# Attention unrolled over all sixteen slots, with the causal mask and the maxima's split on VectorE and the weighing one key step at a time

## The reference

```python
B, T, C = x.shape            # 4, 2048, 256
H, hd, L = 16, 16, 32        # heads, head width, latent width
q, k, v = split(x @ c_attn_w.T + c_attn_b)            # 16 heads of 16
q_lat, k_lat, v_lat = q @ q2l_w.T + b, k @ kv2l_w.T + b, v @ kv2l_w.T + b
q_lat, k_lat = rotary(q_lat), rotary(k_lat)
att = einsum('bhql,bhkl->bhqk', q_lat @ wqk_w.T + wqk_b, k_lat) * L ** -0.5
att = where(causal, att, -inf)
att = softmax(att, axis=-1)  # over the keys
y_lat = einsum('bhqk,bhkl->bhql', att, v_lat)
```

## Time and profile before

| what | value |
|---|---|
| median of three runs | 3400.84 us |
| profiled execution: its time / its span | 3398.39 / 3396.8 us |
| mean granted TensorE clock | 0.946 of full speed |
| `project_heads` | 0 to about 445 us |
| `attend`, first max unit to last turned sums | 466 to 2450 us |
| busy: PE, DVE, ACT, POOL | 90%, 69%, 56%, 23% |
| busy in attention (420 to 2340 us): PE, DVE, ACT, POOL | 96%, 77%, 61%, 9% |

### The profile page before, as it was taken

The page is one execution under the profiler, slowest core; times in us unless marked ns, Lnnn a source line. Parts: engine busy times, 40 slices in busy tenths (PEclk is TensorE's granted clock), DMA queues, the critical chain, the costliest instruction groups (busy, mean ns, idle before and its releaser), DMA issues. The chain is left out here.

```text
span 3396.8 us, 62788 instructions
## 1 busy us (share of the span) xinstructions
PE 3042.3 (90%) x17753; PEld 1998.0 (59%) x17753; DVE 2329.9 (69%) x4664; ACT 1909.4 (56%) x3720; POOL 772.3 (23%) x700
## 2 busy tenths in 40 slices
PE   7888869999999999999999999999889996788780
PEld 6677735555555555555555555555467775677670
DVE  7999977777877877877777777777634443343433
ACT  4566616656666656666656656666545453444434
POOL 6777820000000100000000010000025542222120
PEclk9999959999999999999999999999989998899895
DMA  6666662323322332432333233233283212322215
GB/s 221 219 223 225 216 175 69 72 50 72 71 68 53 73 70 48 95 70 49 72 72 72 48 72 71 54 88 72 51 290 119 92 57 71 90 61 71 43 19 204
DMA packets 254481, 333.42 MB, mean 98 GB/s; under 512 B 57074, under 2 KB 146523, under 8 KB 252896
## 3 DMA queue, kind: packets, MB, share of 16 engines
q1 hardware_dynamic: 236512, 306.49, 31.6%
q0 software_dynamic: 17664, 23.19, 3.6%
HBM read 189.90 MB, written 149.19 MB: 100 GB/s over the span
## 5 line engine op out<-in xcount | busy, mean ns | idle before, releaser
L765 DVE TENSOR_REDUCE att_partial_max<-att_max_bank 128x1 f32<-128x512 f32 (+2 forms) x2640 | 1449.3, 603 | 405.2 <-PE att_max_bank L613 313.3
L728 ACT ACTIVATE att_probs<-att_score_bank 128x512 f32<-128x512 f32 (+3 forms) x2560 | 1203.9, 536 | 745.1 <-PE att_score_bank L653 711.6
L653 PE MATMUL att_score_bank<-att_q_st,att_k_st 98*128 98x512 f32 (+3 forms) x2563 | 1030.4, 407 | 29.7 <-issue 29.7
L613 PE MATMUL att_max_bank<-att_k_st,att_q_st 96*128 96x512 f32 (+2 forms) x2640 | 989.8, 384 | 30.1 <-DVE att_ident_b L757 24.6
L653 PEld LDWEIGHTS att_score_bank<-att_q_st,att_k_st 98*128 98x128 f32 x2563 | 496.3, 194 | 498.1 <-ACT att_probs L728 353.2
L669 PE MATMUL att_acc_bank<-att_probs,att_v_st 128*32 128x512 f32 (+3 forms) x5120 | 605.7, 545 | 0.0
L613 PEld LDWEIGHTS att_max_bank<-att_k_st,att_q_st 96*128 96x128 f32 x2640 | 514.2, 195 | 140.9 <-DVE att_partial_max L765 49.8
L749 POOL TENSOR_SCALAR_AFFINE_SELECT att_probs<-att_probs 128x512 f32<-128x512 f32 x256 | 162.4, 634 | 1818.1 <-ACT att_probs L728 1818.1
L211 POOL TENSOR_TENSOR proj_op_low<-proj_turned,proj_op_high 128x512 fp32r<-128x512 f32 x192 | 274.8, 1461 | 59.0 <-ACT proj_op_high L340 58.6
L616 PE MATMUL att_max_bank<-att_mask,att_ident_b 128*128 128x128 bf16 x1066 | 252.5, 237 | 0.0
L616 PEld LDWEIGHTS att_max_bank<-att_mask,att_ident_b 128*128 128x128 bf16 x1066 | 106.6, 100 | 157.2 <-issue 112.5
(11 more groups left out here) (225 smaller groups left out, 3934.0 us busy)
## 6 DMA issues: line engine op xcount, KB each, us to landing
qk_parts<-proj_parts SPq DMA_DIRECT2D x64, 1024.0 KB, 4.6
att_q_st<-qk_parts SPq DMA_DIRECT2D x204, 256.0 KB, 3.9
att_k_st<-qk_parts SPq DMA_DIRECT2D x204, 256.0 KB, 5.9
att_v_st<-v_tokens SPq DMA_DIRECT2D x68, 256.0 KB, 6.7
v_tokens<-proj_v_tok SPq DMA_DIRECT2D x64, 256.0 KB, 4.5
exp_w<-in_ew SPq DMA_DIRECT2D x16, 1024.0 KB, 9.1
dispatched<-mix_empty_rows SPq DMA_DIRECT2D x8, 1036.0 KB, 15.0
exp_rows<-dispatched SPq DMA_DIRECT2D x16, 518.0 KB, 3.7
```

The costliest lines, as they stand in the source:

```text
L613: last = nc.tensor.matmul(out[:, 0:width], q_st[0:3 * L, c, j, t * P:(t + 1) * P], k_st[0:3 * L, par, kb, j, 0:width], start=True, stop=(k ...
L653: nc.tensor.matmul(score_ps[h % (HG * NK) % 3][:, q0:CH], k_st[:, p, kt // TT, j, (kt % TT) * P:(kt % TT + 1) * P], q_st[:, c, j, q0:CH], ...
L728: nc.scalar.activation(probs[:, k % 4, j, q0:CH], score_ps[(HG * k + j) % 3][:, q0:CH], ACT.Exp).then_inc(exped, 1)
L765: nc.vector.tensor_reduce(partial_max[:, m % 2, j * TT + t, kb:kb + 1], max_ps[max_bank(u)][:, 0:width], AX.X, ALU.max).then_inc(unit_redu ...
```

## The change

In `project_heads` the zeros are no longer written. `attend` is written anew:

- no loop: all 640 key steps of the 16 slots stand in the program one after another, and every wait compares with a constant;
- the mask matmul is gone. A diagonal unit's maximum is taken on VectorE by `tensor_tensor_reduce`, which adds a row of 0 and -1e30 (`edge`) and takes the maximum in one pass. In the program this is two instructions: the pass, and one that writes out the accumulator (128x1);
- the transposition of the maxima by TensorE is gone. VectorE splits (`high_max`, `low_max`) and transposes 32x32 blocks (`turn_max`), one small instruction after each of the next three units, and SP writes the shift by eight DMAs in place of two;
- the max units are dealt by columns: `pace_maxima` lists for each score how many units are issued before it, so that columns of units and columns of scores keep step. 48 units stand before the first score, the lead grows to about 90, and nothing is computed beyond slot 16;
- `weigh(k)` now stands after the third score of step k+1 (`AHEAD = 3`), not after the fourth; `probs` has two buffers, not four; `q_st` is a ring of six chunks; the sums alternate between two banks `acc`, are turned in place and divided from there, and `misc` is gone.

```diff
-KS = [(p, c, kt) for p in range(2) for c in range(NC) for kt in range(TT * (c + 1))]
...
-PER_STEP = MUG // KSG
-LEAD = 5 * HG * TT
...
+KS = [(s, c, kt) for s in range(SLOTS) for c in range(NC) for kt in range(TT * (c + 1))]
+MU = [(s, c, j, t, kb) for s in range(SLOTS) for c in range(NC) for j in range(HG) for t in range(TT) for kb in range(c + 1)]
...
+ACCS = 2
+MAXB = 3
+SCOREB = 3
+PROBS = 2
+QBUF = 6
+AHEAD = 3
+TURN_AFTER = 3
+MARGIN = 20
+FIRST_UNITS = 24
+DIVIDE_BACK = 2
...
+    step = [weight_score(*KS[h // HG]) for h in range(NS)]
+    unit = [weight_unit(*m) for m in MU]
+    rate = sum(unit) / sum(step)
...
+    for h in range(NS):
+        while u < NU and unit_sum[u] < start + rate * step_sum[h]:
+            u += 1
+        due[h] = max(needed[h], min(u, FIRST_UNITS + 2 * h))
...
         @block.tensor
...
-                if kb == c:
-                    last = nc.tensor.matmul(out[:, width - P:width], ident_b[:], mask[:], start=False, stop=True)
...
+            def weigh(k):
...
+                pe.wait_ge(exped, HG * (k + 1))
+                if kt >= TT * c:
+                    pe.wait_ge(masked, n * TT + (kt - TT * c) + 1)
+                if kt == 0 and n >= ACCS:
+                    pe.wait_ge(y_done, n - ACCS + 1)
...
+            pe.wait_ge(consts_in, 32)
             pe.wait_ge(ones_set, 1)
-            with pe.Fori(0, ITS) as it:
...
+            for h in range(NS):
+                while u < MAXIMA_BEFORE[h]:
+                    max_unit(u)
+                    u += 1
+                score(h)
+                while weighed < NK and h == min(HG * PAIR * (weighed // PAIR + 1) + AHEAD, NS) - 1:
+                    weigh(weighed)
+                    weighed += 1
...
         @block.vector
...
+                if kb < c:
+                    nc.vector.tensor_reduce(best, bank[:], AX.X, ALU.max).then_inc(unit_reduced, 1)
+                else:
+                    width = (t + 1) * P
+                    dve.sem_inc(masked_max_due, 1)
+                    nc.vector.tensor_tensor_reduce(
+                        out=edge_sum[:, u % MAXB, 0:width], in0=bank[:, 0:width], in1=edge[:, CH - width:CH], scale=1.0, scalar=LEAST,
+                        op0=ALU.add, op1=ALU.max, accum_out=best).then_inc(unit_reduced, 1)
```

More of the change, by code:

```diff
@@ new lines, in pace_maxima, with weight_unit, weight_score @@
+def pace_maxima():
+    def weight_unit(s, c, j, t, kb):
+        return CH if kb < c else (t + 1) * P
+    def weight_score(s, c, kt):
+        return CH - max(kt - TT * c, 0) * P
+    step = [weight_score(*KS[h // HG]) for h in range(NS)]
+    unit = [weight_unit(*m) for m in MU]
+    rate = sum(unit) / sum(step)
+    needed = [0] * NS
+    for n in range(CHUNKS):
+        for h in range(max(HG * FIRST_STEP[n] - MARGIN, 0), NS):
+            needed[h] = UNITS_THROUGH[n]
+    done, due, ahead = 0, [0] * NS, 0
+    unit_sum = [0]
+    for w in unit:
+        unit_sum.append(unit_sum[-1] + w)
+    step_sum = [0]
+    for w in step:
+        step_sum.append(step_sum[-1] + w)
+    slot = len(KS) // SLOTS * HG
+    start = max(unit_sum[needed[h]] - rate * step_sum[h] for h in range(2 * slot, (SLOTS - 2) * slot))
+    u = 0
+    for h in range(NS):
+        while u < NU and unit_sum[u] < start + rate * step_sum[h]:
+            u += 1
+        due[h] = max(needed[h], min(u, FIRST_UNITS + 2 * h))
+    return due
@@ L564, in _, with turn_after, turned_at, divide_after @@
+        def turn_after(n):
+            return min(weigh_after(n) + TURN_AFTER, NS - 1)
+        def turned_at(h):
+            ends = [n for n in range(CHUNKS) if turn_after(n) == h and weigh_after(n) < NS - 1]
+            return ends[0] if ends else None
+        def divide_after(n):
+            units = MAXIMA_BEFORE[turn_after(n)]
+            return units - DIVIDE_BACK if units < NU else NU + 4
         @block.sync
         def _(sp):
-            for dst, src in loads:
-                sp.dma_start(dst, src).then_inc(consts_in, 16)
@@ new lines, in put_shift, with store_y @@
+            def put_shift(n):
+                sp.wait_ge(rows_ready, n + 1)
+                for part in range(2):
+                    row = q_st[3 * L + part:3 * L + part + 1, n % QBUF].rearrange("w j (t n) -> w (j t) n", n=P)
+                    for at in range(0, P, L):
+                        rows = slice(at + part * HG * TT, at + (part + 1) * HG * TT)
+                        sp.dma_start(row[:, :, at:at + L].bitcast(F32), max_rows[rows, n % 2]).then_inc(shift_in[n % 2], 16)
+            def store_y(n):
+                g, c = divmod(n, NC)
+                b, col = g // G, g % G * (HG * HD)
+                sp.wait_ge(y_done, n + 1)
+                sp.dma_start(d["y"][b, c, :, :, col:col + HG * HD],
+                             y[:, n % 2].rearrange("p t j e -> p t (j e)")).then_inc(y_out[n % 2], 16)
@@ new lines, in turn_sums @@
+            def turn_sums(n):
+                pe.wait_ge(acc_read, n + 1)
+                for t in range(TT):
+                    last = nc.tensor.transpose(acc[n % ACCS][:, t * P:(t + 1) * P], y_raw[:, n % 2, t * P:(t + 1) * P], ident[:])
+                last.then_inc(sums_turned, 1)
+            pe.wait_ge(consts_in, 32)
+            pe.wait_ge(ones_set, 1)
+            u = weighed = 0
+            for h in range(NS):
+                while u < MAXIMA_BEFORE[h]:
[5 more added lines that the diff above has]
+                    weighed += 1
+                n = turned_at(h)
+                if n is not None:
+                    turn_sums(n)
@@ new lines, in _ @@
+            read_next = 0
+            for k in range(NK):
+                g, c, kt = KS[k]
+                q0 = max(kt - TT * c, 0) * P
+                if k >= PROBS:
+                    act.wait_ge(weighted, k - PROBS + 1)
+                for j in range(HG):
+                    act.wait_ge(scored, HG * k + j + 1)
+                    nc.scalar.activation(probs[:, k % PROBS, j, q0:CH], score_ps[(HG * k + j) % SCOREB][:, q0:CH],
+                                         ACT.Exp).then_inc(exped, 1)
+                    if read_next < CHUNKS - 1 and HG * k + j == weigh_after(read_next):
+                        read_acc(read_next)
+                        read_next += 1
@@ new lines, in _ @@
+            divided = 0
+            for u in range(NU + 4):
+                if u < NU:
+                    reduce_unit(u)
+                for stage, later in ((high_max, 1), (low_max, 2), (turn_max, 3)):
+                    if u + 1 - later in UNITS_THROUGH:
+                        stage(UNITS_THROUGH.index(u + 1 - later))
+                if u + 1 in UNITS_THROUGH:
+                    combine_max(UNITS_THROUGH.index(u + 1))
+                while divided < CHUNKS and divide_after(divided) == u + 1:
+                    divide(divided)
+                    divided += 1
@@ L818 @@
+            for n in range(divided, CHUNKS):
+                divide(n)
 EPS = 1e-5
@@ L1784, in const_arrays @@
         "fold8": ((row[:, None] % L) == np.arange(E)[None, :]).astype(f),
-        "mask": np.where(row[None, :] > row[:, None], NEG, 0.0).astype(f),
+        "edge": np.where(np.arange(CH)[None, :] - (CH - P) > row[:, None], NEG, 0.0).astype(f),
     }
```

410 lines of the change are left out of this document (136 added, 274 removed).

## The result

The changed kernel takes 3516 us (median of 4 runs, 3497 to 3539) against 3403 for the kernel before on the same chip: ratio 1.033, interval 1.025 to 1.040. It is slower; the forecast was 3333. The profiled execution is the fastest of the four, 3497.1 us, so the loss to explain there is 98.7 us. The longer runs have a lower mean granted clock (0.929 in the run of 3538.6, 0.944 here), so their spread goes with the clock, to which I come back.

A forecast was written before the change was run, and what follows sets the result against it. PE's program-order queue was taken to set the time (TensorE busy 90% of the span). Terms -55 -92 -11 -16 -3 -38 +115 +30 +5 = -65 took 3398.4 to 3333 us; 8-in-10 range 3265 to 3418.

The forecast's parts named there:

- loop gone: At 7 boundaries between loop turns, PE's 4.60 us stall and the half clock behind it vanish: -55 us.
- masks gone: On PE, 1,024 mask matmuls in 16 slots at 0.09 us each are saved: -92 us (bounds -61 and -128).
- transposes off PE: 66 transpositions of the maxima, 128 columns at 0.16 us each, leave PE: -11 us.
- nothing beyond slot 16, stage end: 80 units past slot 16 dropped, -16 us; stage end no longer waits for a seventeenth slot's loads, -3.
- narrow steps dealt by columns: Narrow diagonal steps stop running at VectorE's pace, units moving at one price per column: 64 chunks x 0.6, -38 us.
- weighing one score earlier: Diagonal weighings make PE wait for POOL, plus score banks: 64 chunks x 1.8, +115 us (bounds 0.9 and 2.3 a chunk).
- masked maxima on VectorE: Masked pass costs a reduction plus 0.15 us accumulator read; PE waits 2 us a slot: +30 us (bounds 0 and +90).
- start: Attention's start: 48 units, then steps without units, then two units a score at VectorE's pace: +5 us.
- Rival 3: VectorE becomes the bound if a diagonal unit takes 0.31 us more; 3460 us at half rate, chance 0.15.
- max units waiting for L729 for more than 60 us in total would make the +30 wrong: Profile sign: PE's max units waiting over 60 us for the masked pass would refute its +30 us term.
- Rival 4: Clock falls in the diagonal: two 0.6 us stands per chunk end cost 1.7 us each, +109, 3442 us; chance 0.08.
- The rule on rates: VectorE's accumulating two-source form halves its rate with two non-bf16 SBUF sources; stays off here, one source being PSUM.

The follow-up runs named there:

- before_unrolled: Kernel before, with its loop over pairs of slots written out for TensorE, ACT, POOL and VectorE; 3349.0 us, ratio 0.984.
- before_no_masks: Kernel before, without the 1024 mask matmuls on TensorE, so diagonal maxima run over unmasked scores; 3323.8 us, ratio 0.976.
- lead_first: late_and_even with the lead of 85 max units laid before the first score in place of 24; 3264.6 us, ratio 0.959.
- columns_lead_first: late_weigh (units still dealt by columns) with 85 max units laid before the first score; 3347.4 us, ratio 0.982.
- even_units: Changed kernel with max units dealt one before each score behind a lead of 85, not by columns; 3367.8 us, ratio 0.989.
- late_and_even: Changed kernel with both edits: weighing behind the fourth score and one max unit before each score; 3290.6 us, ratio 0.965.
- late_weigh: Changed kernel with each step weighed behind the fourth score of the next, not the third (AHEAD 4); 3368.0 us, ratio 0.989.
- plain_maxima: lead_first with diagonal units reduced by the plain maximum, the mask on the maxima left out; 3259.6 us, ratio 0.958.

## Why the prediction was wrong

By its own steps, in the order of the sum:

| step | forecast | measured | by |
|---|---|---|---|
| loop gone | -55 | -55 (-50 in the traces) | before_unrolled |
| masks gone | -92 | -80 | before_no_masks |
| transposes off PE | -11 | not separated | |
| nothing beyond slot 16, stage end | -19 | about -10 | last 40 weighings: 105.2 us in lead_first, 111.6 in before_no_masks; from the last turned sums to the next stage's first matmul 11.1 in place of 15.3 |
| narrow steps dealt by columns | -38 | +83 | columns_lead_first against lead_first |
| weighing one score earlier | +115 | +77 (even dealing), +148 (by columns) | even_units against late_and_even, changed kernel against late_weigh |
| masked maxima on VectorE | +30 | +5 | plain_maxima |
| start | +5 | +21 (by columns), +26 (even dealing) | late_weigh against columns_lead_first, late_and_even against lead_first |

From lead_first one edit at a time leads to the changed kernel, so these terms add up by construction: 3265 + 83 + 21 + 148 = 3516, rounding aside. lead_first itself comes out 15 us above its own sum, which takes the forecast's -11 as it is (3401 - 55 - 80 - 11 - 10 + 5 = 3250); these stay unassigned. The +83 in the place of -38 is 121 of the 183 us that the forecast missed, weighing 33 and start 16.

**The step that failed** is the term "narrow steps dealt by columns", -38, in both its halves. The first is the 0.6 us a chunk that the narrow steps were to stop wasting at VectorE's pace: they became 0.74 shorter, but 0.76 of PE's work had gone out of them, so nothing was saved beyond what was moved. What the first two of the four gained beyond that (0.2), the last two gave back. The second is "what moves are columns: a full step now carries 2,048 of units instead of some 1,740, a narrow one fewer, at one price". Units moved into a full-width step cost 0.34 where the price is 0.13. In lead_first that price holds, as units stand singly and VectorE has room. Rival 3 counted the room over a slot, 93 us of 117, and found plenty. It had to be counted in the step, less the time around the weighing in which VectorE runs dry, and in the order in which the units come: five units (VectorE 2.98 us) take 3.25 if spread and 3.49 if not, six and seven (3.3 us) stay 0.4 us and more above their price even if spread. The forecast saw "three units before one score, with three banks" and charged 2 us a slot; against their price the full-width steps lose 24 x 0.22 = 5.2. Its sign "max units waiting for L729 for more than 60 us in total would make the +30 wrong" came in, at about 150 us between 500 and 2600, but said nothing about the masked pass, which was worth 5: the waits for the plain maxima (L725) are 411 in the same stretch.

**POOL's wait** had the right stands: 0.51 and 0.57 us, where I had worked out 0.6 and 0.65 for the steps of 384 and 256. The count had units in it that covered part of the wait (0.33 and 0.235 at the step of 384), while the same sum took units out of the narrow steps two paragraphs above. With the cover left in, the term is 77; with it taken away, 148, or 2.3 a chunk, the forecast's upper bound. About 22 of the 148 are the clock's and up to 20 the stands behind the turned sums, neither of which was in the count. The two terms were priced apart and are one: the changed kernel's four narrow steps take 11.7 us, even_units' 11.2, with 3.75 units more in them.

**Rival 4** held in part, in the right place: not each of 64 chunks' ends paid, but six, and each about 5 us (31 / 6) where I had 1.7. Of the 148, the clock's share is about (61 - 17) / 2 = 22 us. "No single stand is near 2.57", my reason against it, didn't protect: here two of half a microsecond, 2.6 us apart, were followed by a fall to the same level as 2.57 in the projection. What tells chunks with a fall from the 41 without, at the same pair of stands, is open.

**The rule on rates.** The masked pass reads one PSUM and one SBUF source and took 683 ns, as long as the plain maximum. So far the trace agrees with the Trainium skill (Vector Engine (DVE) Microarchitecture Reference, Points that are easy to get wrong) that the halving is a matter of two SBUF sources. No run here has the pass with two.

**The start:** the forecast priced only VectorE's pace. In the changed kernel's step at 518.20 us PE waits for it while the clock is still at half, until 529 us:

```profile
518.20 0.78 PE L622 MATMUL att_max_bank<-att_k_st,att_q_st 96*128 96x512 f32 x1
519.96 0.80 PE L622 MATMUL att_max_bank<-att_k_st,att_q_st 96*128 96x512 f32 x1 [0.98 <-DVE att_partial_max L725]
```

Two units before each score are units in a row, too. **The tail:** "nothing beyond slot 16" took PE's work out of steps that then wait for the exponentials:

```profile
2541.12 1.07 PE L648 MATMUL att_acc_bank<-att_probs,att_v_st 128*32 128x512 f32 x8
...
2543.30 0.44 PE L634 MATMUL att_score_bank<-att_q_st,att_k_st 98*128 98x384 f32 x1 [0.34 <-ACT att_probs L692]
...
2544.19 1.07 PE L648 MATMUL att_acc_bank<-att_probs,att_v_st 128*32 128x512 f32 x8 [0.45 <-POOL att_probs L711]
```

These steps take 3.07 us with no unit in them; by price they would take at most 2.1 (4 x 0.235 + 1.00 + 0.2).

## What to carry to other kernels

Ask of a second engine not whether it has room in the mean, but whether it has room in the period between two buffer refills: here a fifth unit in a step cost 0.44 us behind another unit and 0.22 by itself, where its columns are worth 0.11, with VectorE busy for 78% of the nine steps shown. Spread the units of the paced engine as evenly as the queue allows, in order and in amount, and don't move work out of a short step before knowing what it covers there. And when two edits touch the same few microseconds, count them in one timeline; apart, one credited the cover that the other had removed. Last, what leaves a step with the work that was moved is no saving: compare a step only with the price of what is left in it.

## What of the hardware was not expected

An accumulator read of 83 ns behind a custom VectorE pass starts together with the next instruction and so costs VectorE almost nothing: the whole masking of 1,024 passes was worth 5 us. Unrolling a loop of 8 turns of 242 us was worth 50 to 55 us; at each of its 7 boundaries PE had stood 4.0 to 4.6 us and then run at half clock for 6.8 or 10.2. And the same pair of 0.5 us stands was followed by half a clock at 6 chunk ends and not at 41 others. The run of 3539 us had a mean clock of 0.929, that of 3497 us 0.944; that such falls made this difference is likely but not shown, as only the shorter one has a trace.
